# Constants, joint compares and bf16 selectors at the ends of three Sturm sweeps; identities added by TensorE

## What is computed

```python
deg = jnp.sum(A, axis=0) + jnp.sum(A, axis=1) - jnp.diagonal(A)
d_inv_sqrt = jnp.where(deg > 0, jax.lax.rsqrt(deg), 0.0)
L_norm = d_inv_sqrt[:, None] * (jnp.diag(deg) - A) * d_inv_sqrt[None, :]
_, U = jnp.linalg.eigh(L_norm)
out = jax.nn.relu(jnp.einsum('mn,bnd->bmd', U.T, h) @ W1 + b1) @ W2 + b2
x = x + jnp.einsum('nm,bmd->bnd', U, out)
```

## Time and profile before

| what | us |
|---|---|
| median of the 3 runs shown | 1697.78 |
| lowest and highest | 1697.2, 1698.26 |
| profiled execution, its own time | 1696.75 |
| span of that execution, first to last instruction | 1694.9 |
| Householder steps | 18 to 788 |
| three sweeps | 797 to 1080 |
| eigenvectors up to the transposes of z | 1080 to 1157 |

### The profile page before, as it was taken

How to read it: one execution, slowest core, us unless ns; L and a number is a source line. 1 busy time by engine, 2 the same in 40 slices (tenths; PEclk the granted TensorE clock), 3 DMA queues, 4 the chain that set the end, 5 groups by cost and what they waited for, 6 DMA issues and landing times.

```text
span 1694.9 us, 25301 instructions
## 1 busy us (share of the span) xinstructions
PE 1286.1 (76%) x5951; PEld 1065.1 (63%) x5954; DVE 1289.3 (76%) x6256; ACT 607.0 (36%) x2109; POOL 400.7 (24%) x2101
## 2 busy tenths in 40 slices
PE   6999999999976667774463434606978899999998
PEld 5777888888855555553342322505657588989897
DVE  7898988888788888888989999984752245555555
ACT  1222222222233443221212222401223377868675
POOL 4333333334445555553101100000000001000000
PEclk9999999999999999999776765757989999999999
DMA  6000000000000000000000000000000000000001
GB/s 162 1 1 1 1 1 1 2 1 1 1 1 1 1 2 1 1 1 1 0 1 0 1 0 1 1 0 1 1 0 1 0 1 1 1 1 26 1 26 50
DMA packets 23401, 12.63 MB, mean 7 GB/s; under 512 B 5075, under 2 KB 22230, under 8 KB 23254
## 3 DMA queue, kind: packets, MB, share of 16 engines
q1 hardware_dynamic: 23254, 11.03, 2.5%
HBM read 6.83 MB, written 4.19 MB: 7 GB/s over the span
## 4 chain that ended last, share of the span: by engine, by line
DVE 48%; PE 32%; issue 9%; POOL 6%; ACT 4%; DVEq 1%; DMA 0%; POOLq 0%
PE bank L800 10%; PE bank L802 6%; DVE A L928 4%; DVE RC L1020 4%; DVE O L1028 3%; PE bank L575 3%; DVE pa L1016 3%; PE bank L578 3%; DVE O L910 3%; DVE O L1024 2%; DVE junk L880 2%; DVE zc L922 2%; DVE wk L914 2%; PE bank L718 2%; PE bank L745 2%
## 5 line engine op out<-in xcount | busy, mean ns | idle before, releaser
L522 ACT ACTIVATE H<-bank,gate_b 128x128 f32<-128x128 f32 (+2 forms) x624 | 213.5, 438 | 81.9 <-PE bank L802 79.3
L578 PEld LDWEIGHTS bank<-O 128*128 128x128 f32 x764 | 201.3, 344 | 0.0
L800 PE MATMUL bank<-O,WlT 128*128 128x128 f32 (+1 forms) x896 | 191.8, 328 | 7.7 <-DVE O L1311 5.6
L587 PE MATMUL bank<-O,y 128*128 128x2 f32 x510 | 142.4, 349 | 65.7 <-DVE y L880 60.3
L575 PE MATMUL bank<-ident,O 128*128 128x128 f32 x382 | 148.2, 457 | 48.1 <-DVE O L910 35.4
L409 ACT ACTIVATE ncp<-pc,RC 128x2 f32<-128x2 f32 (+1 forms) x254 | 74.9, 295 | 291.9 <-DVE RC L901 291.9
L587 PEld LDWEIGHTS bank<-O,y 128*128 128x128 f32 x510 | 128.4, 312 | 77.8 <-issue 72.6
L802 PE MATMUL bank<-H,WlT 128*128 128x128 f32 (+2 forms) x768 | 169.1, 301 | 0.0
L800 PEld LDWEIGHTS bank<-O,WlT 128*128 128x128 f32 x896 | 148.0, 192 | 24.6 <-issue 7.3
L578 PE MATMUL bank<-O 128*128 128x1 f32 x764 | 162.7, 305 | 0.0
L595 PE MATMUL bank<-ident,pc 128*128 128x128 f32 x381 | 147.8, 457 | 5.3 <-DVE pc L899 2.2
(11 more groups left out here) (378 smaller groups left out, 3079.0 us busy)
## 6 DMA issues: line engine op xcount, KB each, us to landing
X<-in_x SPq DMA_DIRECT2D x2, 2048.0 KB, 13.2
out<-X SPq DMA_DIRECT2D x32, 128.0 KB, 1.9
adj_sb<-in_adj SPq DMA_DIRECT2D x1, 256.0 KB, 3.1
W1s<-in_L_gnn_W SPq DMA_DIRECT2D x1, 64.0 KB, 11.1
W2s<-in_L_gnn_W SPq DMA_DIRECT2D x1, 64.0 KB, 4.1
Wg0s<-in_L_gnn_Wg SPq DMA_DIRECT2D x1, 64.0 KB, 3.9
Wg1s<-in_L_gnn_Wg SPq DMA_DIRECT2D x1, 64.0 KB, 3.8
Wl<-in_L_gnn_Wih SPq DMA_DIRECT2D x1, 0.5 KB, 6.8
```

The lines of the kernel that those rows point to most:

```text
L522: ins = a(gates[:, q, i, 0:n], gate_at(p, q, i), fn, bias=gate_b[:, p - 1, i:i + 1])
L578: ins = mm(bank[0][:, 0:1], R[:, b, k, 0:1].to_broadcast([P, P]), R[:, b, k, 0:1], start=(b == bl[0]), stop=(b == 1))
L587: ins = mm(sb_[:, 0:2], y[:, 1:2].to_broadcast([P, P]), R[:, 1, k, :], start=True, stop=(k >= P - 1))
L800: last = mm(gate_at(p, q, i), WlT[:, 0, p - 1, i, :], window(c, p, t, part), start=True, stop=(t == 0))
```

## The change

It has two parts.

At the ends of sweeps: the step of the grid is a number in the program instead of a [128, 1] tile; counts are kept at half their size (`fold`, `tau_row` and `tau_col` are scaled by 0.5 once at the start by GpSimd), so the factors of 2 go; `changes` comes ahead of the sign products; compare and subtraction are one instruction; the last two corrections are added behind the reduction with fused compares; the selectors and the sums for TensorE are bf16; the four lanes are compared by one wide instruction and one reduction; the four `lam` instructions become one. `begin` goes from VectorE to GpSimd (`begin_sweep`, all 128 columns), once before the Householder steps and then behind each of the first two sweeps. TensorE takes the correction twice, since `fold` is halved.

In the WY product: GpSimd no longer makes `IP` nor adds to `Yn`. `mm256` takes a list `plus` of matrices that it adds by products with the identity: `RT` in the even steps 4 to 16, the identity twice in step 18, where the sign of the evacuation moves from `Yn` to `Rm`.

```diff
+            g.tensor_scalar(tau_row[:], junk2[:].rearrange("p b n -> p (b n)"), 0.5, None, ALU.mult).then_inc(S["consts"], 1)
+            g.tensor_scalar(tau_col[:], tau_col[:], 0.5, None, ALU.mult).then_inc(S["consts"], 1)
+            pool.wait_ge(S["consts"], 24)
+            g.tensor_scalar(fold[:], fold[:], 0.5, None, ALU.mult).then_inc(S["consts"], 1)
+            def begin_sweep():
+                for row, rows, val in ((14, 1, 0.0), (15, 1, 1.0), (30, 1, 0.0), (31, 2, 1.0), (33, 1, 0.0)):
+                    ins = g.memset(poly[:, row:row + rows], val)
+                ins.then_inc(S["ring_ready"], 1)
+            begin_sweep()
...
-                elif i < 17 and i % 2 == 1:
-                    r = (i - 3) // 2
-                    pool.wait_ge(act, 5 + 3 * r)
-                    g.tensor_tensor(IP[:], ident[:], Pm[:], ALU.add).then_inc(me, 1)
-                elif i == 18:
-                    pool.wait_ge(act, 27)
-                    g.tensor_tensor(Yn[:], Yn[:], ident[:], ALU.add).then_inc(me, 1)
-                    pool.wait_ge(me, 12)
-                    g.tensor_tensor(Yn[:], Yn[:], ident[:], ALU.add).then_inc(me, 1)
...
             for i in range(1, 22):
                 wy(i)
+                if i in (2 * NCH, 4 * NCH):
+                    s = i // (2 * NCH)
+                    pool.wait_ge(S["corr_ready"], s)
+                    pool.wait_ge(S["sgn_ready"], 2 * NCH * s)
+                    begin_sweep()
...
+            def mm256(dst, L, R, plus=()):
                 for m in range(NB):
                     for b in range(NB):
+                        last = mm(bank[dst][:, m * N:(m + 1) * N], L[:, b, m * P:(m + 1) * P], R[:, b, :], start=(b == 0), stop=(b == 1 and not plus))
+                    for i, M in enumerate(plus):
+                        last = mm(bank[dst][:, m * N:(m + 1) * N], idf, M[:, m, :], start=False, stop=(i + 1 == len(plus)))
                 return last
...
-                        mm256(3, IP, RT).then_inc(me, 1)
+                        mm256(3, Pm, RT, plus=(RT,)).then_inc(me, 1)
...
-                    mm256(2, MT, Rm).then_inc(me, 1)
+                    mm256(2, MT, Rm, plus=(ident, ident)).then_inc(me, 1)
...
                         pe.wait_ge(S["corr_ready"], s + 1)
-                        mm(bank[0][:, 0:w], fold[:].rearrange("p a r -> p (a r)"), corr[:, 0:w], start=False, stop=False)
+                        for o in range(2):
+                            mm(bank[0][:, 0:w], fold[:].rearrange("p a r -> p (a r)"), corr[:, 0:w], start=False, stop=False)
...
+                        mm(bank[7][:, j * P:j * P + w + 1], ind0[0:ROWS, j * P:(j + 1) * P], sums_b[0:ROWS, 0:w + 1], start=True, stop=True)
+                        last = mm(bank[7][:, j * P + w + 1:j * P + w + 2], ind1[0:ROWS, j * P:(j + 1) * P], sums_b[0:ROWS, w:w + 1], start=True, stop=True)
...
-                    link(ts(step, step, 1.0 / f, None, ALU.mult))
-                    for j in range(LANES):
-                        ins = ts(lam[:, j * f:(j + 1) * f], fine[:, 0:f], step, lo[:, j:j + 1], ALU.mult, ALU.add)
-                    link(ins)
+                    step = step / f
+                    link(stt(out=by_lane, in0=fine[:, 0:f].unsqueeze(1).to_broadcast([P, LANES, f]), scalar=step,
+                             in1=lo[:].unsqueeze(2).to_broadcast([P, LANES, f]), op0=ALU.mult, op1=ALU.add))
...
+                changes(2 * (s + 1) * NCH - 1, w)
                 tt(pb2[:, 0, 0:w], x_ab[:, 0], x_ab[:, 1], ALU.mult)
                 link(tt(pb2[:, 1, 0:w], x_ab[:, 0], poly[:, 31, 0:w], ALU.mult))
                 dve.wait_ge(S["ends_in"], s + 1)
+                ts(pb2[:, 0, 0:w], pb2[:, 0, 0:w], 0.0, None, ALU.is_gt)
                 link(tt(pb2[:, 1, 0:w], pb2[:, 1, 0:w], ends[:, 1, 0:w], ALU.mult))
-                ts(pb2[:, 0, 0:w], pb2[:, 0, 0:w], 0.0, 2.0, ALU.is_gt, ALU.mult)
-                link(ts(pb2[:, 1, 0:w], pb2[:, 1, 0:w], 0.0, 2.0, ALU.is_gt, ALU.mult))
-                tt(corr[:, 0:w], pb2[:, 1, 0:w], pb2[:, 0, 0:w], ALU.subtract).then_inc(S["corr_ready"], 1)
-                changes(2 * (s + 1) * NCH - 1, w)
-                if s + 1 < SWEEPS:
-                    begin(WIDTH[s + 1])
+                stt(out=corr[:, 0:w], in0=pb2[:, 1, 0:w], scalar=0.0, in1=pb2[:, 0, 0:w], op0=ALU.is_gt, op1=ALU.subtract).then_inc(S["corr_ready"], 1)
...
-                link(tt(m0, m4, m2, ALU.mult))
-                link(ts(m1, m0, 0.0, 2.0, ALU.is_gt, ALU.mult))
-                link(ts(m2, m3, 0.0, 2.0, ALU.is_gt, ALU.mult))
-                link(tt(m3, m1, m2, ALU.subtract))
+                tt(m0, m4, m2, ALU.mult)
...
-                link(tt(shift_sum[:, 0:w], shift_sum[:, 0:w], m3, ALU.add))
+                link(stt(out=total, in0=m3, scalar=0.0, in1=total, op0=ALU.is_gt, op1=ALU.subtract, reverse1=True))
+                link(stt(out=total, in0=m0, scalar=0.0, in1=total, op0=ALU.is_gt, op1=ALU.add))
                 if s == 0:
-                    link(ts(ind1, tau, shift_sum[:, w - 1:w], None, ALU.is_gt))
-                    link(ts(ind0, tau, shift_sum[:, 0:1], None, ALU.is_gt))
+                    link(ts(ind1, tau_row[:], shift_sum[:, w - 1:w], None, ALU.is_gt))
+                    ts(ind0, tau_row[:], shift_sum[:, 0:1], None, ALU.is_gt)
+                    v.tensor_copy(sums_b[:, 0:w], total)
+                    link(v.memset(sums_b[:, w:w + 1], 1.0))
                     tt(ind0, ind0, ind1, ALU.subtract).then_inc(S["loc_in"], 1)
...
+                    link(tt(junk3, found[:, :, 0:w], tau_col[:].unsqueeze(2).to_broadcast([P, LANES, w]), ALU.is_lt))
+                    link(v.tensor_reduce(cnt[:], junk3, AX.X, ALU.add))
+                    link(tt(cnt[:], cnt[:], found[:, :, w], ALU.mult))
+                    link(stt(out=cnt[:], in0=found[:, :, w + 1], scalar=float(w), in1=cnt[:], op0=ALU.mult, op1=ALU.add))
                 else:
-                    for j in range(LANES):
-                        link(ts(junk3[:, j, 0:f], shift_sum[:, j * f:(j + 1) * f], tau_col[:, j:j + 1], None, ALU.is_lt, ALU.add, accum_out=cnt[:, j:j + 1]))
+                    link(tt(junk3[:, :, 0:f], total.rearrange("p (q i) -> p q i", q=LANES), tau_col[:].unsqueeze(2).to_broadcast([P, LANES, f]), ALU.is_lt))
+                    link(v.tensor_reduce(cnt[:], junk3[:, :, 0:f], AX.X, ALU.add))
```

More of the change, by code:

```diff
@@ L133, in gnn_kernel @@
         poly = o_rows[:, 0:23].rearrange("p r (i w) -> p (r i) w", w=PTS)
-        ind0, ind1 = (m[:].rearrange("p r n -> p (r n)") for m in (below, A))
+        ind0, ind1 = (chg[:, 0, i:i + 4].rearrange("p i w -> p (i w)") for i in (0, 4))
         unit_row = ones[:, 0:PTS]
@@ L653, in _ @@
                         for o in range(2):
-                            last = mm(bank[6 + o][:, 0:2 * w], sel[:, o].rearrange("p a r -> p (a r)"), ends[:, :, 0:w], start=True, stop=True)
-                        last.then_inc(S["ends_ps"], 1)
+                            mm(bank[6 + o][:, 0:2 * w], sel[:, o].rearrange("p a r -> p (a r)"), ends[:, :, 0:w], start=True, stop=True).then_inc(S["ends_ps"], 1)
                         pe.wait_ge(S["corr_ready"], s + 1)
-                        mm(bank[0][:, 0:w], fold[:].rearrange("p a r -> p (a r)"), corr[:, 0:w], start=False, stop=False)
+                        for o in range(2):
+                            mm(bank[0][:, 0:w], fold[:].rearrange("p a r -> p (a r)"), corr[:, 0:w], start=False, stop=False)
                     pe.wait_ge(S["chg_ready"], n + 1)
@@ L667, in _ @@
                     for j in range(LANES):
-                        mm(bank[7][:, j * P:j * P + w + 1], ind0[0:ROWS, j * P:(j + 1) * P], shift_sum[0:ROWS, 0:w + 1], start=True, stop=True)
-                        last = mm(bank[7][:, j * P + w + 1:j * P + w + 2], ind1[0:ROWS, j * P:(j + 1) * P], ones[0:ROWS, 0:1], start=True, stop=True)
+                        mm(bank[7][:, j * P:j * P + w + 1], ind0[0:ROWS, j * P:(j + 1) * P], sums_b[0:ROWS, 0:w + 1], start=True, stop=True)
+                        last = mm(bank[7][:, j * P + w + 1:j * P + w + 2], ind1[0:ROWS, j * P:(j + 1) * P], sums_b[0:ROWS, w:w + 1], start=True, stop=True)
                     last.then_inc(S["loc_ps"], 1)
@@ L952, in _ @@
             link(ts(bnd[:, 3:4], bnd[:, 1:2], bnd[:, 7:8], -0.005 * SPAN, ALU.mult, ALU.add))
-            link(v.memset(bnd[:, 4:5], 1.01 * SPAN / (ROWS * WIDTH[0])))
-            step = bnd[:, 4:5]
+            step = 1.01 * SPAN / (ROWS * WIDTH[0])
             link(stt(out=bnd[:, 5:6], in0=bnd[:, 1:2], scalar=-1.0, in1=bnd[:, 0:1], op0=ALU.mult, op1=ALU.max))
@@ L976, in pair @@
                 return poly[:, ring_u(j):ring_v(j) + 1:ring_v(j) - ring_u(j), 0:w]
-            def begin(w):
-                for row, rows, val in ((14, 1, 0.0), (15, 1, 1.0), (30, 1, 0.0), (31, 2, 1.0), (33, 1, 0.0)):
-                    ins = v.memset(poly[:, row:row + rows, 0:w], val)
-                return mark(ins)
             for s in range(SWEEPS):
@@ L1074, in _ @@
```

(23 more changed lines are left out.)

34 lines of the change are left out of this document (16 added, 18 removed).

## The result

The changed kernel takes 1676.64 us in the median of 4 runs (1676.14 to 1677.8), the kernel before 1697.49 us beside it (4 runs); the ratio is 0.9878, interval 0.9861 to 0.9895. That is 20.85 us less.

What follows compares the result with a forecast made beforehand. VectorE was taken to bound the kernel between 788 and 1157 us. Gains of 7.05 + 0.68 + 6.63 + 2.49 + 0.95 - 0.4 = 17.4 us gave 1680.4 us, range 1677.2 to 1684.0 us.

Steps and rivals of the forecast that it cites:

- up to the reduction: Sweep ends, until VectorE's reduction starts: gains of 1.57, 1.57 and 0.57 us in sweeps 0, 1 and 2.
- locating products: End of sweep 0, TensorE: 16 fp32 instructions of 3.57 us become 8 bf16 ones of 1.1 us, gain 2.47 us.
- Stalls of the recurrence: Sturm sweeps: seven VectorE steps stretched by GpSimd's identity adds return to usual durations, gain 7.05 us in all.
- TensorE's added products at nought: Even WY steps: extra fp32 identity products, +1.7 us per step and +3.4 in step 18, hidden, so no cost.
- Start and preparation: Ring memsets leave VectorE ahead of sweep 0, gain 0.68 us; GpSimd's added start work costs VectorE 0.4 us.
- Compares and constants behind the reductions: Ends of sweeps 1 and 2, behind the reduction: shorter VectorE work gains 0.92 and 0.38 us.
- Selectors, compare and new grid in sweep 0: Sweep 0, behind the reduction: gains of 0.19 us to the selectors, 1.54 for compare and new grid, 0.86 for step and lam.
- (a): Sweep ends: relocated GpSimd memsets hold VectorE, 0.9 us at two sweep ends, 1682.2 us; chance 0.08.
- (c): Recurrence: ScalarE's evacuations cause the stretched steps, so the 7.05 us stay, 1687.4 us; chance 0.05.
- (d): Sweeps: TensorE's eight fuller steps become the bound, VectorE waits for chg products, slower, 1702 us; chance 0.01.
- (b): Ends of sweeps 1 and 2: TensorE stays at high clock, reductions up to 1.15 and 0.55 us earlier, 1678.7 us; chance 0.12.

Runs made afterwards that it cites:

- second record: The changed kernel, unaltered, run once more on the chip of the three runs beside it: 1678.29 us (4 runs, ratio 0.9884).
- WY half alone: The kernel before with only the WY product's identities added by TensorE, sweep ends as before: 1689.48 us against 1697.78 us.
- the two GpSimd runs: The changed kernel plus seven unused GpSimd instructions where line 336 stood: adds reading SBUF, 1685.09 us; memsets of as many columns, 1677.68 us.
- runs with memsets: The changed kernel plus seven GpSimd memsets of 512 columns, which only write, where line 336 stood: 1677.68 us.
- tripled identity: The changed kernel with TensorE adding RT three times instead of once in the seven even steps: 1678.11 us against 1678.29 us.
- fp32 selectors: The changed kernel with fp32 selectors, threshold row and sums instead of bf16: 1681.04 us, ratio to the kernel before 0.9901.

## Why the prediction was wrong

The direction and most of the mechanisms held. Two terms of the sum failed: "up to the reduction", 3.71 us forecast and 4.87 measured, and "locating products", a gain of 2.47 us forecast and 3.09 measured. With smaller misses 17.4 us was 2.6 us too little for the touched part (20.0 us in the first record, 19.4 in the second). The median lies 3.8 us below the forecast; of the other 1.1 us half is in the parts whose code is the same, and half comes from the median lying 0.5 us above the recorded execution here and 1.03 us above it in the forecast. Term by term:

- **Stalls of the recurrence**, 7.05 forecast: 7.16 in the whole, 7.12 for the WY half alone. Right, and the cause is shown by the two GpSimd runs.
- **TensorE's added products at nought**: right; the room was larger than said, since 7.3 us took the low clock for the whole step, and the clock rises within it.
- **Start and preparation**, 0.68 - 0.4 forecast: 0.61 - 0.08. The instruction at 13.38 us took 0.51 instead of 0.43 us beside GpSimd's scaling of tau_row, which lasted 1.50 us; whether GpSimd waited in it isn't shown. GpSimd's added work there took 3.4 us (12.11 to 15.51 us) where some 2.2 were forecast, and was covered all the same.
- **Up to the reduction**, 1.57, 1.57, 0.57 forecast (3.71): 2.11, 1.91, 0.85 (4.87). This is the first step that failed, in sweep 0 for the wait, in sweeps 1 and 2 for the overlap. In sweep 0 the text says of `down` that "nothing moves that". TensorE's clock does: in the first record the odd step ended early and nothing waited, 0.54 us more than forecast; in the second record the wait was there and the gain was 1.42. In sweeps 1 and 2 I laid two passes of the corrections end to end ahead of the chg products, 0.45 and 0.4 us. The chg products start 0.18 and 0.10 us behind the first of them, since the passes overlap: 0.27 and 0.30 us, about the whole miss of 0.34 and 0.28. That TensorE is late next there was right, with 0.81 us of idle time against 1.2 forecast.
- **Locating products**, 1.1 us forecast with 0.9 as the lower bound: 0.52 us from the first product to VectorE, a gain of 3.09 us (from 3.61) instead of 2.47. The eight follow each other at 0.02 to 0.06 us. This is the second step that failed: my lower bound was the duration of a lone weight load, but durations overlap and only the distance of starts adds up. So the bound itself was wrong.
- **Compares and constants behind the reductions**: 0.92 and 0.38 forecast in sweeps 1 and 2, 1.02 and 0.70 measured. I priced the fused compares like line 1078 (0.28 us at 64 columns), which has a [128, 1] scalar. With a constant they take 0.22 to 0.23; `lo` fell from 0.22 to 0.16 us. The step's constants were costed only where an instruction vanished.
- **Selectors, compare and new grid in sweep 0**, gains of 0.19, 1.54 and 0.86 forecast: 0.30, 1.54 and 0.77, with 0.05 more on the steps between. Right, and the 0.35 us for a bf16 selector, a choice between two bounds, was met by luck.
- **What was left out of the range**: parts whose code is the same differ from record to record. Over all kernels here the Householder part took 768.6 to 769.4 us and the part behind the eigenvectors 537.8 to 540.4 us. The first record of the changed kernel holds the shortest of the latter, 0.65 us less than the kernel before. The second measurement gave 1678.29 us, within the range, 18.85 us less than before. So half a microsecond outside the range is less than what such parts scatter, and which side of it the time fell on is luck; the 2.6 us in the touched part are not.

The rivals: (a), (c) and (d) are excluded by the runs with memsets, with WY alone and with the tripled identity. (b) came true in part: in 2 of 9 records with that order (fp32 selectors, tripled identity) the products at the end of sweep 1 ran at the high clock, worth 0.89 us; in the other seven they ran at the low one, and at the end of sweep 2 in all nine (1.04 us for two, reduction 0.25 us late). Its reason, more work in the sweep, isn't shown. The 1702 us of rival (d) is a slip: 1697.8 and 3.4 us make 1701.2.

## What to carry to other kernels

When an engine is never idle and bounds the stage, look for instructions that are longer than their neighbours of the same line, and for a GpSimd instruction that reads SBUF and starts just ahead of them; moving such work to an engine with time to spare pays about the GpSimd instruction's length less what VectorE would have done. Price a run of short matmuls by the distance of their starts, not by durations. Cut both traces at the same instructions before judging a difference of a microsecond in a kernel of 1700: the whole time scatters by more, while the touched stretches repeat to some hundredths, but for the ones that wait for TensorE, which its clock moves by 0.7 to 0.9 us.

## What the runs showed of the hardware

- A GpSimd add with both inputs in SBUF stretched one VectorE instruction that started behind it by about 1.0 us (seven whose results nobody uses: 7.1 us). Six of the seven had two tensor inputs, one had a single one (1.14 against 0.19 us). Where VectorE's instruction started first, by 0.14 us, the add took 1.68 us instead and VectorE lost nothing. Seven memsets of the same size cost nothing.
- Eight bf16 products with 64 rows and at most 65 columns, weights changing each time, took 0.5 us from the first to VectorE's next step; 16 fp32 instructions of the same work 3.6 us.
- A VectorE instruction with two tensors and a scalar took about 0.06 us less with a constant than with a [128, 1] scalar (0.22 against 0.28 at 64 columns, 0.16 against 0.22 at 4).
- TensorE's fp32 instruction of 256 columns took 0.43 us at the low and 0.22 us at the high clock, and when it rose within the last odd step of sweep 0 differed between two executions of one kernel (5.2 and 6.0 us for the step).
